# Position attention: negated maxima moved by DMA into rows of the query stack, maxima of two heads at once over bank pairs

## The reference, cut to what matters

```python
def _L1_xattn_ref(q, k, v, gamma):          # q = x, k = v = ctx_2048: 64 x 64 x 256
    qh = q.reshape(B, 8, 8, 256); kh = k.reshape(B, 8, 8, 256); vh = v.reshape(B, 8, 8, 256)
    qk = jnp.einsum('bhdq,bhdl->bhql', qh, kh) * 8 ** -0.5
    sm = jax.nn.softmax(qk, axis=-1)
    return gamma * jnp.einsum('bhql,bhdl->bhdq', sm, vh).reshape(B, 64, 256)
x = _layernorm(x + _L1_xattn_ref(x, ctx_2048, ctx_2048, gamma))
```

## Time and profile before

| | |
|---|---|
| median of 3 runs | 5420.6 us (5417.31 to 5425.5) |
| profiled execution | 5410.26 us, span 5408.5 us |
| PE busy over the span | 4780.6 us (88%) |
| DVE busy | 3370.1 us (62%) |
| ACT busy | 2107.8 us (39%) |
| POOL busy | 1577.4 us (29%) |
| mean granted TensorE clock | 0.962 |

### The profile page before, as it was taken

One profiled execution on the slowest core, in us unless ns is written; L12 is line 12 of the kernel. 1 busy time (PEld: TensorE's weight loads), 2 busy tenths in 40 slices (PEclk: granted clock), 3 DMA queues, 4 the chain that ended last, 5 costly groups with the idle time before them and its releaser, 6 DMA issues.

```text
span 5408.5 us, 85898 instructions
## 1 busy us (share of the span) xinstructions
PE 4780.6 (88%) x31749; PEld 3347.2 (62%) x31749; DVE 3370.1 (62%) x6404; ACT 2107.8 (39%) x4198; POOL 1577.4 (29%) x3211
## 2 busy tenths in 40 slices
PE   8998898699997898885599999999997999999788
PEld 6775888366665677774266666666664565656455
DVE  4557327577767668887655555555554666666698
ACT  3444113255543333332244444444442334333222
POOL 1111003433321233332233333333332323223122
PEclk9998999799998999997699999999998999999899
DMA  1002000333320000001100000000001000000000
GB/s 40 1 1 85 20 1 6 92 77 76 76 52 30 4 6 8 8 8 67 43 1 1 1 1 1 1 1 1 1 1 34 5 6 6 5 6 4 3 14 16
DMA packets 106062, 109.22 MB, mean 20 GB/s; under 512 B 12144, under 2 KB 98352, under 8 KB 101168
## 3 DMA queue, kind: packets, MB, share of 16 engines
q1 hardware_dynamic: 105648, 103.72, 7.4%
HBM read 86.90 MB, written 16.78 MB: 19 GB/s over the span
## 4 chain that ended last, share of the span: by engine, by line
PE 49%; DVE 19%; issue 14%; POOL 9%; ACT 5%; DMA 3%; SPq 1%; POOLq 0%; DVEq 0%; ACTq 0%
PE banks L2198 12%; PE banks L2349 4%; POOL factors L2709 4%; PE banks L718 3%; PE banks L1752 3%; PE banks L2334 2%; DMA stack<-parts_x 2%; PE banks L478 2%; PE banks L2207 2%; PE banks L1163 2%; PE banks L745 2%; DVE neg_max L1076 1%; DVE stats L257 1%; PE banks L1662 1%; PE banks L2217 1%
## 5 line engine op out<-in xcount | busy, mean ns | idle before, releaser
L263 POOL TENSOR_TENSOR var_eps<-mean_var,ln_eps 128x1 f32<-128x1 f32 x384 | 83.1, 216 | 1716.2 <-DVE mean_var L259 1171.9
L1076 DVE TENSOR_REDUCE neg_max<-banks 128x2 f32<-128x512 f32 x512 | 343.4, 682 | 184.0 <-PE banks L1066 177.7
L1193 ACT ACTIVATE exps<-banks 128x512 f32<-128x512 f32 x512 | 304.7, 597 | 304.0 <-PE banks L1147 286.7
L2243 DVE TENSOR_REDUCE square_sums<-squares 128x4 f32<-128x512 f32 x256 | 174.7, 682 | 258.0 <-ACT squares L2235 254.1
L246 ACT COPY xT<-banks 128x256 f32<-128x256 f32 x160 | 59.8, 374 | 559.7 <-PE banks L238 369.1
L2256 POOL TENSOR_TENSOR factors<-mean_squares,minus_half 128x4 f32<-128x4 f32 x256 | 258.3, 1009 | 21.3
L2198 PE MATMUL banks<-wq,xT 128*128 128x512 f32 x512 | 245.9, 603 | 14.9 <-ACT xT L246 14.9
L1752 PEld LDWEIGHTS banks<-yT,w_swiglu 128*128 128x128 f32 x2048 | 238.5, 193 | 30.2 <-issue 29.9
L1752 PE MATMUL banks<-yT,w_swiglu 128*128 128x128 f32 x2048 | 247.4, 277 | 8.6 <-DVE hidden L1776 8.6
L1066 PE MATMUL banks<-stack,stack 128*128 128x256 bf16 x1024 | 202.2, 281 | 59.3 <-DMA stack<-parts_x 53.9
L1146 PE MATMUL banks<-stack,stack 128*128 128x256 bf16 x1024 | 252.5, 274 | 1.6 <-ACT exps L1193 1.2
(11 more groups left out here) (377 smaller groups left out, 12105.1 us busy)
## 6 DMA issues: line engine op xcount, KB each, us to landing
contextT<-in_ctxT SPq DMA_DIRECT2D x96, 128.0 KB, 3.2
parts_context<-parts SPq DMA_DIRECT2D x96, 64.0 KB, 2.0
parts_x<-parts SPq DMA_DIRECT2D x96, 64.0 KB, 2.0
stack<-parts_context SPq DMA_DIRECT2D x32, 192.0 KB
stack<-parts_x SPq DMA_DIRECT2D x32, 192.0 KB
x_all<-in_x SPq DMA_DIRECT2D x1, 4096.0 KB, 14.2
context<-in_ctx SPq DMA_DIRECT2D x64, 64.0 KB, 2.2
context<-in_ctx SPq DMA_DIRECT2D x32, 128.0 KB, 2.3
```

Of the source, the lines that this page charges most:

```text
L1076: v.tensor_reduce(self.mx[s][:, :, g:g + 1], self.bM[g % 2].rearrange("p (h c) -> p h c", h=DH), AX.X, ALU.max, negate=True).then_inc(self ...
L1193: self.nc.scalar.activation(self.e[n % 8][:], self.bE[n % 2].rearrange("p (l c) -> p l c", l=DH), ACT.Exp, scale=self.TOK ** -0.5).then_in ...
```

## The change

The matmul with the selection matrix goes, and its constant with it. In its place three rows, 48 to 50, of the query stack are filled with the three parts of the negated maxima by three DMAs a tile, issued by SP in a new phase that stands ahead of the stack's; rows 32 to 63 of the key stacks are set to 1.0 once. The maxima use rows 0 to 47, the scores rows 0 to 63. The maxima of two heads are taken by one DVE instruction over two banks. The banks are given out anew: the transpose shares the two banks of the scores in a rotation of 17 slots. Scores start at tick 10 instead of 6, `weigh` is issued in halves, the reciprocal in halves, and the output moves to lag 6.

```diff
-    STEP, SCORES_FROM = 16, 6
+    STEP, SCORES_FROM, TURN_AT = 16, 10, 4
+    ROWS, MAX_ROWS = 48, 64
+    TURN_SLOT = STEP - SCORES_FROM + TURN_AT
-        self.sel = w("select", [P, self.HEADS, P], BF16); self.load(self.sel[:], p.ins["c_select"])
-        self.bM, self.bN, self.bE, self.bO = (B[0], B[1]), B[2], (B[3], B[4]), (B[5], B[6])
+        self.bM, self.bE, self.bO = (p.ps[:, 0:2, :], p.ps[:, 2:4, :]), (B[4], B[5]), (B[6], B[7])
 def setup_pool:
         for i in (0, 1):
             for n in range(self.STACK_BUFFERS):
-                pool.memset(self.kq[i][n][:].bitcast(I32), 0)
+                last = pool.memset(self.kq[i][n][:].bitcast(I32), 0)
+        last.then_inc(self.zeroed.sem, 1)
+        pool.wait_ge(self.zeroed.sem, self.zeroed.at(1))
+        for n in range(self.STACK_BUFFERS):
+            last = pool.memset(self.kq[0][n][32:self.MAX_ROWS], 1.0)
 def max_pe:
+            i = g // 2
+            if g % 2 == 0:
+                if i >= 2:
+                    pe.wait_ge(self.maxed.sem, self.maxed.at(t, i - 1))
+                elif begun(t - 1):
+                    pe.wait_ge(self.maxed.sem, self.maxed.at(t - 1, 8 + i - 1))
             for h in range(DH):
-                last = ...matmul(self.bM[g % 2][:, h * D:(h + 1) * D], q[:, g, h * P:(h + 1) * P], k[:, g, :], start=True, stop=True)
-            last.then_inc(self.made.sem, 1)
+                last = ...matmul(self.bM[i % 2][:, g % 2, h * D:(h + 1) * D], q[rows, g, h * P:(h + 1) * P], k[rows, g, :], start=True, stop=True)
+            if g % 2 == 1:
+                last.then_inc(self.made.sem, 1)
 def max_dve:
-        for g in range(self.HEADS):
-            dve.wait_ge(self.made.sem, self.made.at(t, g + 1))
+        for i in range(8):
+            yield
+            dve.wait_ge(self.made.sem, self.made.at(t, i + 1))
-            v.tensor_reduce(self.mx[s][:, :, g:g + 1], self.bM[g % 2]..., AX.X, ALU.max, negate=True)
+            v.tensor_reduce(self.mx[s][:, :, 2 * i:2 * i + 2]..., self.bM[i % 2]..., AX.X, ALU.max, negate=True)
             yield
 def turn_max_pe:
-        for _ in range(4):
+        for _ in range(self.TURN_AT):
             yield
         pe.wait_ge(self.m_split.sem, self.m_split.all(t))
+        self.slot_free(pe, self.turn_slot(t))
+    def move_max_sp(self, sp, t, s):
+        sp.wait_ge(self.m_copied.sem, self.m_copied.all(t))
+        for j in range(3):
+            sp.dma_start(self.stack(1, t)[self.ROWS + j:self.ROWS + j + 1, :, :],
+                         self.mT[s][32 * j:32 * j + self.HEADS, :]).then_inc(self.m_moved.sem(t), 16)
 def score:
         if n == 0:
-            pe.wait_ge(self.m_copied.sem, self.m_copied.all(t))
+            pe.wait_ge(self.m_moved.sem(t), self.m_moved.all(t))
         for l in range(DH):
-            self.nc.tensor.matmul(out, k[:, h, l * P:(l + 1) * P], q[:, h, :], start=True, stop=False)
-            last = self.nc.tensor.matmul(out, self.sel[:, h, :], self.mT[s][:], start=False, stop=True)
+            last = ...matmul(self.bE[self.slot(t, n) % 2][:, l * D:(l + 1) * D], k[rows, h, l * P:(l + 1) * P], q[rows, h, :], start=True, stop=True)
+    def weigh_at(self, pe, t, s, tick):
+        r, after = divmod(tick - self.SCORES_FROM - 5, 4)
+        if 0 <= r < 4 and after % 2 == 0:
+            self.weigh(pe, t, s, r, after // 2)      # one half: the matmuls with l = 0, then with l = 1
 def out_dve:
-        for _ in range(9):
-            yield
+        yield
+        yield
         dve.wait_ge(self.weighed.sem, self.weighed.all(t))
-        v.reciprocal(self.rd[:], self.bO[s][:, D:2 * D]).then_inc(self.o_read.sem, 1)
+        for half in (0, 1):
+            at = slice(half * P, (half + 1) * P)
+            v.reciprocal(self.rd[:, at], self.bO[s][:, D + half * P:D + (half + 1) * P]).then_inc(self.o_read.sem, 1)
+            yield
+            yield
 def programs:
-            "pe": [[(5, self.score_late_pe), (4, self.score_pe), (4, self.turn_max_pe), (3, self.max_pe)]],
+            "pe": [[(6, self.weigh_last_pe), (5, self.score_late_pe), (4, self.score_from_pe), (4, self.turn_max_pe), (3, self.max_pe)]],
-            "dve": [[(4, self.split_max_dve), (5, self.out_dve), (3, self.max_dve)]],
-            "pool": [(3, self.values_pool), (5, self.tail_pool), (1, self.split_pool)],
-            "sp": [(2, self.stack_sp), (1, self.parts_sp), (0, self.source_sp)],
+            "dve": [[(4, self.split_max_dve), (6, self.out_dve), (3, self.max_dve)]],
+            "pool": [(3, self.values_pool), (6, self.tail_pool), (1, self.split_pool)],
+            "sp": [(4, self.move_max_sp), (2, self.stack_sp), (1, self.parts_sp), (0, self.source_sp)],
```

More of the change, by code:

```diff
@@ L1058, in max_pe @@
         k, q = self.stack(0, t), self.stack(1, t)
+        rows = slice(0, self.ROWS)
         pe.wait_ge(self.stacked.sem(t), self.stacked.all(t))
         for g in range(self.HEADS):
[L1061 to L1064, removed]
+            i = g // 2
[4 more added lines that the diff above has]
+                    pe.wait_ge(self.maxed.sem, self.maxed.at(t - 1, 8 + i - 1))
             for h in range(DH):
-                last = self.nc.tensor.matmul(self.bM[g % 2][:, h * D:(h + 1) * D], q[:, g, h * P:(h + 1) * P], k[:, g, :], start=True, stop=True)
-            last.then_inc(self.made.sem, 1)
+                last = self.nc.tensor.matmul(self.bM[i % 2][:, g % 2, h * D:(h + 1) * D], q[rows, g, h * P:(h + 1) * P], k[rows, g, :], start=True, stop=True)
+            if g % 2 == 1:
+                last.then_inc(self.made.sem, 1)
             yield
@@ L1095, in split_max_dve, with slot, turn_slot, slot_free @@
         v.tensor_copy(m3(2), self.m2[:]).then_inc(self.m_split.sem, 1)
+    def slot(self, t, n):
+        return (self.HEADS + 1) * t.index + n + (1 if n >= self.TURN_SLOT else 0)
+    def turn_slot(self, t):
+        return (self.HEADS + 1) * (t.index - 1) + self.TURN_SLOT
+    def slot_free(self, eng, slot):
+        t, n = divmod(slot - 2, self.HEADS + 1)
+        if slot < 2 or (n == self.TURN_SLOT and t + 1 >= self.NT):
+            return
+        if n == self.TURN_SLOT:
+            eng.wait_ge(self.m_copied.sem, self.m_copied.all(Tile(t + 1)))
+        else:
+            eng.wait_ge(self.exped.sem, self.exped.at(Tile(t), n + 1 - (1 if n > self.TURN_SLOT else 0)))
     def turn_max_pe(self, pe, t, s):
-        for _ in range(4):
+        for _ in range(self.TURN_AT):
             yield
         pe.wait_ge(self.m_split.sem, self.m_split.all(t))
-        if begun(t - 1):
-            pe.wait_ge(self.m_copied.sem, self.m_copied.all(t - 1))
-        turned = self.bN[:].bitcast(BF16)
+        self.slot_free(pe, self.turn_slot(t))
+        turned = self.bE[self.turn_slot(t) % 2].bitcast(BF16)
         for h in range(DH):
@@ L1112, in copy_max_act @@
         if begun(t - 2):
-            act.wait_ge(self.scored.sem, self.scored.all(t - 2))
-        self.nc.scalar.copy(self.mT[s][:], self.bN[:].bitcast(BF16)[:, 0:D]).then_inc(self.m_copied.sem, 1)
+            act.wait_ge(self.m_moved.sem(t - 2), self.m_moved.all(t - 2))
+        self.nc.scalar.copy(self.mT[s][:], self.bE[self.turn_slot(t) % 2].bitcast(BF16)[:, 0:D]).then_inc(self.m_copied.sem, 1)
+    def move_max_sp(self, sp, t, s):
[3 more added lines that the diff above has]
+                         self.mT[s][32 * j:32 * j + self.HEADS, :]).then_inc(self.m_moved.sem(t), 16)
     def values_pool(self, pool, t, s):
@@ L1136, in score, with weigh @@
         if n == 0:
-            pe.wait_ge(self.m_copied.sem, self.m_copied.all(t))
+            pe.wait_ge(self.m_moved.sem(t), self.m_moved.all(t))
             if first(t):
                 pe.wait_ge(self.loaded.sem, self.loaded.done)
[L1140 to L1143, removed]
+        self.slot_free(pe, self.slot(t, n))
+        rows = slice(0, self.MAX_ROWS)
         for l in range(DH):
-            out = self.bE[n % 2][:, l * D:(l + 1) * D]
-            self.nc.tensor.matmul(out, k[:, h, l * P:(l + 1) * P], q[:, h, :], start=True, stop=False)
-            last = self.nc.tensor.matmul(out, self.sel[:, h, :], self.mT[s][:], start=False, stop=True)
+            last = self.nc.tensor.matmul(self.bE[self.slot(t, n) % 2][:, l * D:(l + 1) * D], k[rows, h, l * P:(l + 1) * P], q[rows, h, :], start=True, stop=True)
         last.then_inc(self.scored.sem, 1)
-    def weigh(self, pe, t, s, r):
+    def weigh(self, pe, t, s, r, l):
         pe.wait_ge(self.exped.sem, self.exped.at(t, 4 * r + 4))
-        if r == 0:
+        if r == 0 and l == 0:
             pe.wait_ge(self.v_ready.sem, self.v_ready.all(t))
@@ L1156, in weigh @@
                 pe.wait_ge(self.o_read.sem, self.o_read.all(t - 2))
-        for part in range(4):
-            l, ones = divmod(part, 2)
+        for ones in (0, 1):
             for g in range(4):
@@ L1162, in weigh, with score_from_pe, score_late_pe, weigh_last_pe @@
                 out = self.bO[s][32 * g:32 * g + 32, ones * D:(ones + 1) * D]
```

(31 more changed lines are left out.)

26 lines of the change are left out of this document (16 added, 10 removed).

## The result

The changed kernel takes 5758.15 us, the median of 4 runs (5756.39 to 5767.81), against 5418.95 us before: 1.0624 times as long, 95% interval 1.0609 to 1.0638. The direction was forecast, the size was not: +339 us where +48 stood, outside the range of 5424 to 5500.

A forecast was written before the change was run, and what follows sets the result against it. PE and the chain through the stack's DMA were both within a us of the 19.30 us step. Steps +39.7, drain -5.4 and setup +13.8 gave +48 us, so 5469 us, range 5424 to 5500.

The forecast's parts named there:

- rival B: PE's clock stays down for longer, or PE idles again before recovery: some 1.7 us more a step, 5520 us; chance 0.10.
- the term for the clock: Half clock on PE after each idle piece, in ticks 0 to 4: 1.15 us a step, bounds 0 and 4.05.
- the loop of copy, moves and stack: PE to the transpose, copy, SP's three moves, then the stack PE needs at the next tick 0: 19.35 us a step.
- the moves' issue: SP issuing the three DMAs ahead of the stack: 1.35 us a step, from a span of 1.1 to 1.95.
- The second loop: POOL's values after the weigh at tick 13, tail, split, parts, stack: 37.9 us for two steps, 18.95 each.
- PE's step: PE's own work in a step without the select matmuls and with weighs in halves: 15.6 us.
- Memsets: Four setup memsets of 32 partitions x 4096 bf16 in POOL's chain ahead of the first split: 13.8 us, or 7.
- The moves land: Landing of the moved maxima, 2.2 us, hidden: in place 8.7 us into the step, PE at tick 10 at 9.8.
- Reductions: DVE's 16 reductions a step become 8 over 1024 elements, 1207 ns each: 10.9 becomes 9.7 us, no gain by itself.
- Drain: From the last maxima step to the stage's end: 49.3 us before, 43.9 after, so -5.4.
- A: Rival with no clock loss: a step of 19.35 us, +6 to +12.5, so 5426 to 5433 us; chance 0.22.
- C: Rival where the stack lands 3 us sooner: a step of 17.5 us, -43, so 5378 us; chance 0.10.

The follow-up runs named there:

- e5: Kernel before the change with every bf16 matmul of the stage on at most 64 rows (maxima 48, scores 64, select 64): 5433.61 us, 1.0024 times before.
- e6: Changed kernel with 128 rows in maxima and scores, SP issuing the stack ahead of the moves: 5743.59 us, 1.0605 times before.
- e7: Changed kernel with 128 rows, stack issued ahead of the moves, POOL's order split, tail, values, and key-stack ones set as int32: 5366.95 us, 0.9907 times before.
- all-rows run: Changed kernel with all 128 rows of the stacks in the maxima and score matmuls, added rows zero: 5485.02 us, 1.0113 times before.
- e10: Kernel before the change with its bf16 matmuls on at most 64 rows and its weighs in halves two ticks apart: 5965.18 us.
- e4: Kernel before the change with maxima cut to 48 rows and scores to 64, select matmuls still at 128: 5657.10 us.

## Why the prediction was wrong

**The failed step is the return of the clock.** "PE has 15.6 us of dense work after each idle piece, and the rows come back to 1.00 within 7": so it stood against rival B, and the term for the clock had its upper bound in the 4.05 us of ticks 0 to 4. All rows behind it were of matmuls on 128 rows. The stage starts at half clock, as before (0.50 from 950 to 1000 us in both). In the kernel before it rises at 1009 us, among matmuls on 128 rows; in the changed kernel dense work on 48 and 64 rows, with the weighs in halves, doesn't bring it back. The whole step, 15.6 us by my sum, goes at half clock: 2 x 15.6 = 31.2, measured 30.15. The upper bound of the term should have been this, 10.8 us above the loop's 19.35 and not 4.05. The Trainium skill (TensorE: Matmul & The Clock Gate, What's actually happening) tells the clock by how busy TensorE has been; here it was busy for 99.66 of 100 us and stayed at 1.2 GHz. The measurement decides: being busy isn't enough.

**"Nothing below hangs on it" was the sentence that hid it.** It was said of the 48 and 64 rows, with only their duration in mind. The duration was right (0.108 us in e5). The clock hung on them, together with the halves of the weighs, which I had priced at four switches a step.

**The loops were right and hidden.** In the change PE at half clock is slower than every loop. With all rows the loop of copy, moves and stack is there with 19.31 us for 19.35, and the kernel takes 5485 us where 5469 stood. What is off in it is the moves' issue, 1.92 for 1.35, and the mean loss of clock, 21.0 - 19.3 = 1.7 a step for 1.15. The second loop showed in e6, where it closed into one step; the forecast had it only with moves that don't wait for the stack. That both loops are what kept the gain away is shown by e7, which cuts them and runs at PE's pace. I had PE's step there at 15.6; it is 16.96, since a half weigh and its switches take longer than 1.05 us a pair of ticks, and PE waits for the copy of the maxima (0.46 us in one step).

**The small terms.** Memsets 13.8 forecast, 13.86 measured; as int32 7.04, so POOL pays by element. The moves land in 1.8 us where 2.2 stood. Reductions 1207 ns forecast, 1226 measured, and DVE is nowhere near the bound. Drain: -5.4 forecast, +16.7 measured, for the same reason as the steps. Of the rivals, A's step of 19.35 us is seen in single steps of the all-rows run (19.31), not in the changed kernel. B, the clock that stays down, was the right direction: it had 1.7 us a step above the forecast's 20.5, measured 9.65, and it still tied the loss to the idle pieces. C had nothing for it: from the stack's first issue to PE's start it is 12.33 us in the all-rows run, and C wanted 3 us less than 12.84. That the time came out slower, as forecast, is no credit to the mechanism: the loop that was to make it so is hidden.

## What to carry to other kernels

A matmul that uses fewer rows costs the same time at the same clock (0.108 us on 64 and on 128 rows), but it isn't the same to the clock: before cutting rows, or splitting up what stands between the few-row matmuls, ask what will raise the stage's clock, and hold the case "the whole stage at half clock" as a price. In a program woven by hand, a new wait at tick k on a queue puts everything behind it on that queue k ticks later; follow what is behind it to its consumer, around the loop. And a small DMA issued behind a large one on the same queue can land as late as the large one (8.77 us in e6), so it must be ordered by when each is needed.

## What the runs showed of the hardware that was not expected

- TensorE stayed at 1.2 GHz from 1100 to 1900 us while busy for 99.66 to 99.74 us of every 100 (100.00 in e10), with bf16 matmuls on 48 and 64 rows and weighs in halves; zeros in the added rows brought it to 2.4 GHz for most of the time.
- The clock fell with TensorE never idle (18 times in e4 from 1100 to 1700 us), in stretches of bf16 matmuls of which two in three were on 48 or 64 rows, and rose again in or right behind whole weighs.
- Alternating 64-row and 128-row matmuls are 0.21 us apart at full clock, 0.108 without the alternation; 48 and 64 rows alternate without that cost (e5: 0.11 us from one to the next).
- A memset on POOL of 32 x 4096 bf16 takes 3.47 us, of the same bytes as int32 1.76 us.
- Three moves of 8 KB each into one partition land 1.8 us after issue in the median when nothing is queued ahead of them (the changed kernel), up to 9.3 us behind a stack (e6).
